# Graph network on one core: SyncE fetches one gathered column in three groups, row by row; ScalarE issues the stream loads

## The reference

```
# layer 0, transformer convolution, twice (passes c1, c2)
score = sum(q[dst] * (k[src] + e)) / 8 ; a = softmax over the edges of one dst
out   = segment_sum(a * (v[src] + e), dst) + x @ ws + bs
# layers 1 and 2, graph attention, 4 heads and 1 head (passes c3, c4, c5)
e = leaky_relu(alpha_s[src] + alpha_d[dst] (+ edge term in c3)) ; w = softmax over one dst
out = segment_sum(w * h[src], dst)
# layer 3, principal neighbourhood aggregation (pass c6)
u = h[src] + edge_attr_64 ; mean, max, min, std of u over the edges of one dst
```

## Time and profile before

| what | us |
|---|---|
| median of 3 runs | 13507.51 |
| their range | 13507.29 to 13508.39 |
| span of the profiled execution, first to last instruction | 13480.4 |
| GpSimd busy in it | 10010.5 |
| VectorE busy | 6813.4 |
| ScalarE busy | 4134.7 |

### The profile page before, as it was taken

How to read it: one execution, slowest core, us unless ns; L and a number is a source line. 1 busy time by engine, 2 the same in 40 slices (tenths; PEclk the granted TensorE clock), 3 DMA queues, 4 the chain that set the end, 5 groups by cost and what they waited for, 6 DMA issues and landing times. The chain is left out here.

```text
span 13480.4 us, 46161 instructions
## 1 busy us (share of the span) xinstructions
PE 515.1 (4%) x1768; PEld 338.5 (3%) x1768; DVE 6813.4 (51%) x10542; ACT 4134.7 (31%) x4038; POOL 10010.5 (74%) x10585
## 2 busy tenths in 40 slices
PE   3000001100000300000010000000000000000001
PEld 1000000100000200000000000000000000000000
DVE  2787776477777433333333333343333335656566
ACT  4333333233333312222212222211111113666663
POOL 7777777777777677777777777777777776777775
PEclk9999999555555655555555555555555555555555
DMA  8444443344444222222212222222222222444443
GB/s 328 128 126 119 119 119 100 95 119 119 120 120 120 57 66 63 63 61 63 60 47 59 59 58 59 59 48 57 59 59 59 58 59 82 159 159 157 159 153 121
DMA packets 919562, 1312.58 MB, mean 97 GB/s; under 512 B 600892, under 2 KB 616404, under 8 KB 906113
## 3 DMA queue, kind: packets, MB, share of 16 engines
q0 software_dynamic: 341536, 381.76, 15.7%
q10 hardware_dynamic: 85680, 537.82, 10.2%
q1 hardware_dynamic: 492209, 391.76, 10.1%
HBM read 651.09 MB, written 659.48 MB: 97 GB/s over the span
## 5 line engine op out<-in xcount | busy, mean ns | idle before, releaser
L1767 POOL DMA_INDIRECT c_y<-g_tab,srcs x4689 | 4426.0, 944 | 1429.0 <-issue 1376.9
L2200 POOL DMA_INDIRECT c_y<-h_tab,srcs x1563 | 1474.8, 944 | 510.8 <-issue 466.5
L741 POOL DMA_INDIRECT c_y<-h_tab,srcs x1563 | 1474.9, 944 | 476.3 <-issue 476.3
L1796 DVE TENSOR_TENSOR c_s<-c_y,c_ad 128x64 f32<-128x64 f32 (+1 forms) x297 | 79.1, 266 | 3450.0 <-DMA c_y<-g_tab,srcs 3448.7
L741 POOL DMA_INDIRECT first_y<-h_tab,srcs x1483 | 1399.3, 944 | 452.9 <-issue 451.7
L1879 ACT ACTIVATE c_ex<-c_de 128x64 f32<-128x64 f32 (+1 forms) x297 | 67.4, 227 | 2321.1 <-DVE c_de L1827 2320.0
L1840 DVE TENSOR_TENSOR_SCAN c_acc<-c_r,c_w_in 128x1156 f32<-128x1156 f32 (+1 forms) x297 | 753.0, 2535 | 23.2
L763 DVE TENSOR_TENSOR_SCAN c_q_all<-c_mask,c_q_in 128x408 f32<-128x408 f32 (+2 forms) x792 | 734.0, 995 | 17.8 <-issue 10.5
L806 DVE TENSOR_TENSOR_SCAN c_acc<-c_r,c_w_in 128x408 f32<-128x408 f32 (+2 forms) x792 | 731.1, 986 | 8.2
L839 ACT ACTIVATE c_q_in<-c_q_raw 128x1552 f32<-128x1552 f32 (+1 forms) x198 | 596.2, 3011 | 195.8 <-DVE c_q_in L822 195.8
L1893 ACT ACTIVATE c_row<-c_acc 128x1088 f32<-128x1088 f32 (+1 forms) x297 | 617.7, 2080 | 0.0
(11 more groups left out here) (402 smaller groups left out, 6461.6 us busy)
## 6 DMA issues: line engine op xcount, KB each, us to landing
rows_d<-c_row ACTq DMA_DIRECT2D x97, 2048.0 KB, 6.9
rows_d<-c_row ACTq DMA_DIRECT2D x291, 576.0 KB, 2.9
rows_d<-c_row ACTq DMA_DIRECT2D x194, 784.0 KB, 3.4
c_q_raw<-q_start SPq DMA_DIRECT2D x194, 776.0 KB, 4.5
q_start<-first_y SPq DMA_DIRECT2D x97, 776.0 KB, 9.0
c_y<-g_tab,srcs POOLq DMA_INDIRECT x4689, 2.5
c_y<-h_tab,srcs POOLq DMA_INDIRECT x3126, 2.5
c_ea<-in_edge_attr SPq DMA_DIRECT2D x97, 512.0 KB
```

The costliest lines, as they stand in the source:

```text
L741: nc.gpsimd.indirect_dma_start(y[:, g % NY, k, 0:D], None, h_tab, source(g, k))\
L1767: nc.gpsimd.indirect_dma_start(y[:, b, k, :], None, g_tab, source(g, k))\
L2200: nc.gpsimd.indirect_dma_start(y[:, b, k, :], None, h_tab, source(g, k))\
```

## The change

- **Fetched rows.** A new class `SyncRows`. In groups 2, 5, 8, ... 95 (slots 2 and 5 of six) the last of the 16 columns is left out of GpSimd's list; in c6 only in slot 5, so in one group of six. SyncE fetches that column with 128 DMAs, one for each row, whose byte offset in the table is in a register. It reads the offsets from a small tile `at`, 32 at a time, into registers. The tile is loaded from `places_d` in DRAM, one column ahead (in c6 after the column). VectorE waits for these rows as well (`arrived`). In c1, group 2 is still fetched by GpSimd in `begin`.
- **The table of offsets.** `begin` loads the 32 columns of `src` that are fetched this way, multiplies them by 256 and by 288 (three more VectorE steps), and stores both to `places_d`.
- **Stream loads.** All of SyncE's stream loads in the passes are issued by ScalarE, between its own steps. SyncE keeps the load of `ad_raw` at the start of c3 to c5.
- **Row buffers.** c3 to c6 use six slots where they had two, and VectorE's loop runs over six groups.

The core of the diff:

```diff
+EVERY, SYNC_K = NY // 2, GW - 1
+SYNC_SLOTS, NSYNC = [EVERY - 1, NY - 1], NGRP // EVERY
+NREG = 32
+def by_pool(g, taken):
+    return width(g) - taken.count(g % NY)
+def fill_of(slot, taken):
+    return 16 * (H2 if slot == HALVED else GW - taken.count(slot))
+    class SyncRows:
+        def load_places(self, sp, n, b):
+            sp.dma_start(self.at[b:b + 1, :], places_d[bass.ds(n * 2 + b + self.table * NSYNC, 1), :])\
+                .then_inc(self.at_loaded.h, 16)
+        def column(self, sp, n, b, used, more=True):
+            sp.wait_ge(*self.at_loaded((n + 1 if self.single else n * 2 + b + 1 - self.first) * 16))
+            if more and not self.single:
+                self.load_places(sp, n + b, 1 - b)
+            if not isinstance(n, int) or n:
+                sp.wait_ge(*used[SYNC_SLOTS[b] % 2]((n - 1) * (NY // 2) + SYNC_SLOTS[b] // 2 + 1))
+            sp.nop(nofuse=True)
+            rows = self.tab.rearrange("n f -> (n f)").bitcast(U8)
+            for lo in range(0, P, NREG):
+                _, places = nc.values_load_multi_w_load_instructions(
+                    self.at[b:b + 1, lo:lo + NREG], [mybir.EngineType.SP], min_val=0, ...)
+                for p, place in enumerate(places, lo):
+                    sp.dma_start(self.y[p:p + 1, SYNC_SLOTS[b], SYNC_K, 0:self.width].bitcast(U8),
+                                 rows[bass.ds(place, 4 * self.width)].rearrange("(a n) -> a n", a=1))\
+                        .then_inc(self.got[b].h, 16)
+            if more and self.single:
+                self.load_places(sp, n + 1, b)
+        def arrived(self, v, slot, n):
+            if slot in SYNC_SLOTS and SYNC_SLOTS.index(slot) in self.got:
+                b = SYNC_SLOTS.index(slot)
+                v.wait_ge(*self.got[b]((n + 1 - (b < self.first)) * (16 * P)))
...
 begin, SyncE
+                    sp.dma_start(src_i[:], a["src"].rearrange("(p t) -> t p", p=P)
+                                 [EVERY * GW - 1:EVERY * GW * NSYNC:EVERY * GW, :]).then_inc(src_loaded.h, 16)
...
+                sp.wait_ge(*vs.upto(len(vs)))
+                for n in range(2):
+                    sp.dma_start(places_d[n * NSYNC:(n + 1) * NSYNC, :], places[:, n, :]).then_inc(places_stored.h, 16)
+                sp.wait_ge(*places_stored(32))
 each pass, SyncE: the stream loads go
+                by_sync.all_columns(sp, weighted)
 each pass, GpSimd
-                    for k in range(width(g)):
+                    for k in range(by_pool(g, taken)):
 c3 to c6, GpSimd
-                    if g >= 2:
-                        pool.wait_ge(*weighted[b](g // 2))
+                    if g >= NY:
+                        pool.wait_ge(*weighted[g % 2]((g - NY) // 2 + 1))
 each pass, VectorE
+                    by_sync.arrived(v, slot, use)
 c1 and c2, ScalarE
+                def next_operands(n, j, w=GW):
+                    i, b = n * (NY // 2) + j // 2, j % 2
+                    act.wait_ge(*weighted[b](i))
+                    act.wait_ge(*q_turned[b](i))
+                    operands(n, j, w)
+                def group(n, j):
+                    pc = piece(n * (NY // 2) + j // 2, j % 2)
+                    turn(pc)
+                    send(piece(n * (NY // 2) + (j + 1) // 2 - 1, 1 - j % 2))
+                    next_operands(n + (j + 1) // NY, (j + 1) % NY)
+                    weights(pc)
 c3, ScalarE
+                def group(i, b, next_w=GW):
+                    weights(piece(i, b))
+                    if bd is not None:
+                        act.wait_ge(*e_scored[b](i + 1))
+                        edge_attrs(i + 1, b, next_w)
+                    send(piece(i, b))
 c6, ScalarE
+                def next_attrs(i, b, w=GW):
+                    act.wait_ge(*lifted[b](i))
+                    edge_attrs(i, b, w)
 c3 to c6
-        y = st.sb("y", [P, 2, GW, TG])
+        y = st.sb("y", [P, NY, GW, TG])
```

More of the change, by code:

```diff
@@ L187, in wide_slots, with row_slots, pass_slots @@
         return [make(f"{name}{b}", each * ((NWBLK + 1 - b) // 2)) for b in range(2)]
[L189 to L195, removed]
+    def row_slots(self, fills, taken=(), cut=0):
+        return [[self.dma(f"gathered_{slot}{part}", fill_of(slot, taken) * n - cut * part)
                  for part in range(1 + (slot == HALVED))] for slot, n in enumerate(fills)]
+    def pass_slots(self, taken, ahead=0):
+        return self.row_slots([len(range(slot, NGRP, NY)) - (slot < ahead) for slot in range(NY)], taken, CUT)
     def dma_slots(self, name, total):
@@ L360, in _ @@
                 sp.dma_start(prev_i[:], a["dst"][0:EP].rearrange("(p t) -> p t", p=P)).then_inc(dst_loaded.h, 16)
+                with nc.allow_non_contiguous_dma("one column of src in three groups"):
+                    sp.dma_start(src_i[:], a["src"].rearrange("(p t) -> t p", p=P)
+                                 [EVERY * GW - 1:EVERY * GW * NSYNC:EVERY * GW, :]).then_inc(src_loaded.h, 16)
                 sp.wait_ge(*zeroed(1))
@@ L691, in conv_edges @@
         q_loaded, e_loaded = (st.dma_slots(n, 16 * HALF) for n in ("q_loaded", "e_loaded"))
-        gathered = st.row_slots([len(range(slot, NGRP, NY)) - (slot < ahead) for slot in range(NY)], CUT)
+        taken = SYNC_SLOTS
+        gathered, by_sync = st.pass_slots(taken, ahead), SyncRows(st, y, h_tab, D, 0, ahead // EVERY)
         q_turned, weighted, row_ready = (st.piece_slots(n) for n in ("q_turned", "weighted", "row_ready"))
@@ L770, in step @@
                     for part in halves(gathered[slot], pc):
-                        v.wait_ge(*part((use + (slot >= ahead)) * ((8 if slot == HALVED else 16) * GW) - missing(pc)))
+                        v.wait_ge(*part((use + (slot >= ahead)) * fill_of(slot, taken) - missing(pc)))
+                    by_sync.arrived(v, slot, use)
                     v.wait_ge(*e_loaded[pc.slot](pc.load * 16 + 16))
@@ L874, in _ @@
                 weights(piece(0, 0))
[L875 to L884, removed]
+                for j in range(1, NY):
+                    group(0, j)
+                with act.Fori(1, NGRP // NY) as n:
+                    for j in range(NY):
+                        group(n, j)
                 for before, pc in zip([piece(HALF - 2, 1)] + LASTS, LASTS):
@@ L1728, in gat_edges @@
             eadded = st.sem("eadded", NPIECE)
-        gathered = st.gather_halves(f"gathered_{'first' if tag in ('c1', 'c2', 'c3') else 'later'}_", 8 * GW * HALF)
+        taken = SYNC_SLOTS
+        gathered, by_sync = st.pass_slots(taken), SyncRows(st, y, g_tab, TG, 1)
         weighted, row_ready, den_in = (st.piece_slots(n) for n in ("weighted", "row_ready", "den_in"))
@@ L1793, in step @@
                     w_heads = w_cur.rearrange("p (h j) t -> p h j t", h=H)
-                    for part in halves(gathered[pc.slot], pc):
-                        v.wait_ge(*part(pc.load * (8 * GW) + 8 * GW - missing(pc)))
+                    for part in halves(gathered[slot], pc):
+                        v.wait_ge(*part((use + 1) * fill_of(slot, taken) - missing(pc)))
+                    by_sync.arrived(v, slot, use)
                     v.tensor_tensor(s0[:, :, 0:w], ys[:, :, D:D + H].rearrange("p t h -> p h t"), ad[:, :, cols],
@@ L2166, in pna_edges @@
         e_loaded = st.dma_slots("e_loaded", 16 * HALF)
-        gathered = st.gather_halves(f"gathered_{'first' if tag in ('c1', 'c2', 'c3') else 'later'}_", 8 * GW * HALF)
+        taken = SYNC_SLOTS[1:]
+        gathered, by_sync = st.pass_slots(taken), SyncRows(st, y, h_tab, D, 0, single=True)
         row_stored = st.store_slots("row_stored")
```

162 lines of the change are left out of this document (85 added, 77 removed).

## The result

The changed kernel takes 13300.6 us (median of 4 runs, 13275.6 to 13302.8); the kernel before, beside it on the same chip, 13507.4 (4 runs, 13504.6 to 13508.4). The ratio is 0.9843, with a 95% interval of 0.9829 to 0.9857. The medians differ by 206.8 us, the profiled spans (13480.4 and 13273.9) by 206.5; 214.5 had been forecast, and 13293 as the time. The time of a run lies 1.7 us above its own span (13275.6 and 13273.9), so of the 27.1 us between the span and the median before, some 25 are the difference between one execution and another; here too the profiled execution is the fastest, 25 us under the median.

The account below looks back on a forecast made before the run. GpSimd's gathers, 1.2485 us a column, were taken to bound the kernel. 218.5 us saved less 4 us of setup gave 214.5, so 13266 us against the profiled span, 13293 with 27.1 us added for the median; range 13280 to 13880.

Parts of the forecast that it names:

- S: SyncE's time for one fetched column: 52.5 + 4 + 0.7 = 57.2 us, bounds 41.5 and 75.0.
- The gain: GpSimd's list in c1 to c6: 175 columns fewer at 1.2485 us, 218.5 us saved.
- Setup: Setup stage: SyncE's 4096-word load of one src column in three groups adds 4 us, bounds 0 and 15.
- A row: One-row DMA on SyncE: 0.34 + 0.06 + 0.01 = 0.41 us, bounds 0.32 and 0.52; 128 rows 52.5 us.
- rival D: Both register instructions per row make SyncE the bound in five passes: 1590 us more, 14883 us; chance 0.20 with milder forms.
- Register loads: SyncE reading 128 places into registers, four times 32: 4 us a column, between 0.1 and 7.7.
- The limit: c1 to c5: GpSimd needs 58.7 us for 47 columns; a fetch within that costs nothing.
- under its wait for GpSimd: VectorE's one more wait, in a third of its steps, was to lie under its existing wait for GpSimd.
- The other sign: Sign of being right: SyncE's idle time ended by VectorE's weighted in each column.
- Rival C: c1 and c2: ScalarE's loads hold SyncE three times 3.4 us a column, adding 542 us, 13835 us; chance 0.12.
- The bound from above: c6: SyncE has 117 us for a fetched column, so S does not matter even at 75 us.
- The price of a miss: c1 to c5: each us of S above 58.7 costs 159 us.

Follow-up runs that it names:

- the one with exchanged pieces: Changed kernel with c1/c2 edge features in 128 pieces (not 2048) to a spare tile, c6's store in 4096 pieces (not 128): 13275.6 us, one run.

## Why the prediction was right

The mechanism was the one forecast: GpSimd's pace sets the passes, 175 columns less at 1.2485 us, and the fetch lies beside. The time was met to 0.06%, the gain to 4% (206.8 us of 214.5). Two terms of S were not, their errors had opposite signs, and S left out two more. The lower bound of S was also added up wrongly: 41.0 + 0.1 + 0.7 is 41.8, not 41.5; nothing rests on it.

**The gain.** 218.5 us were forecast off GpSimd's list, 214 measured between the first and the last gather. Of that, 2.3 us came back behind the last gather of c1 and 3.9 behind that of c6 (a wait of 25.7 us where it was 21.8), where the last group waits for VectorE and its store. Setup cost 1.2 us (c1's first gather starts at 391.8 instead of 390.6), not the 4 that I took; its bounds of 0 and 15 hold it. 214 - 6.2 - 1.2 = 206.6; measured 206.5. So what was left out are the ends of the passes, 6.2 us, which no row of before had suggested; they are as long without any fetch, so they aren't SyncE's doing. With all columns back on GpSimd the wait of c1 is 19.8 us and that of c6 21.1, so the one comes with the moved loads or buffers and the other with GpSimd's shorter list.

**A row.** 0.317 us was measured, outside my bounds of 0.32 to 0.52 and well below the 0.41 taken. I had the MOVE right (one, no FUSED_REGOPS, so rival D's premise is refuted), but took 0.34 us as the issue from loads of 2 KB. The one-row load with its 0.28 us was the nearest row of all and pointed lower; the real figure is 0.225. 128 rows are 40.6 us, not 52.5.

**Register loads.** Four of 2.12 us are 8.5 us, above my upper bound of 7.7. The bound assumed one MOVE for a value, 0.06 us, and forgot that the load can have a part beside it that doesn't depend on the number. The Trainium skill ("DMA: Bandwidth & Descriptors", "Latency and other measured facts") gives a floor of about 600 ns. The trace doesn't contradict a floor (the shortest load took 0.97 us, for 16 values), but as a price it is far off: four floors are 2.4 us, less than a third of what was measured; the price follows the number of values in the two sizes tried.

**What S left out.** Once in two columns the loop goes back to its start and 2.4 us pass without an instruction (in the timeline above, 3054.39 to 3057.22 between a fetch and the next load, against 0.3 us inside the body); in c1 it is 3.7 to 5.2 us. And 3.7 to 4.5 us a column in c1 and c2 go to row issues that take 1 us instead of 0.225 while ScalarE's DMAs move. So S came out as 40.6 + 8.5 + 4 + 1.2, and some 3 us of loads and waits, 57.6 in c1 and 57.2 in c2, in place of 57.2. The sum was right by luck: the rows were 12 us too dear, and 4.5 us of register loads, the branch and the slow issues that I had left out made up for them.

**The limit.** 58.7 us was right for c2 to c5, where c2 has 1.5 us of margin and c3 to c5 some 5: a period there is 56.5 us, of which 2.9 are waits (276.5 us over 96 columns), so SyncE's own work is 53.6. In c1 it was wrong: there it is 57.5, since five groups lie ready, and the change has nothing to spare. A forecast that had counted this would have given c1 a chance of its own to lose. The forecast's "under its wait for GpSimd" failed there: VectorE waits for SyncE's rows in 27 columns of 31. That it costs nothing measurable is shown by the kernel without fetches and by the one with exchanged pieces. The other sign, that idle time of SyncE ends by `weighted` in each column, came in 57 columns of 96 in c3 to c5, in all but one of c6, and in 3 of 63 in c1 and c2.

**Rival C.** The hold-up does reach from ScalarE's queue to SyncE's. The Trainium skill ("DMA: Bandwidth & Descriptors", "Queues, rings and completion order") has it that the two engines have no descriptor generator of their own, and the trace agrees in the sign. What failed in C is the size: not 3.4 us for each load of 2048 pieces, but some 1.4 us a group with all of ScalarE's DMAs counted, because SyncE isn't stopped, it goes on at about 1 us a row. The other way nothing is seen. ScalarE's own issue of that load takes 1.084 us, where SyncE's took 0.38 us, but it takes 1.075 us too in the kernel in which SyncE issues no row, so SyncE's rows aren't the cause, and what is stays open:
```profile
L900 ACTq DMA_DIRECT2D c_y<-in_edge_attr x98: 457/1075/1120, 2488.0 to 4388.9; - x98
```
I had read the earlier trace rows as weak evidence against a hold behind the 2 MB store: a single issue, with none behind it. In the changed kernel, where rows follow each other, the issues behind the same store are slow for 6.4 us, and 3.4 of them are lost.

**The bound from above.** In c6 the forecast said that S doesn't matter even at 75 us, and the measured 63.4 us in a period of 118 agrees (the 117 us of the forecast should have been 95 x 1.2485 = 118.6). Tried at three groups it did matter, which shows why a column in six was the right share there.

**The price of a miss.** 159 us for each us of S stands: 9.1 us more of register loads (9.3 in the periods of c1 and c2, 10.2 in c3 to c5), less a margin of some 1 us in c1, 1.5 in c2 and 5 in c3 to c5, gave 974 us, which is 6.1 x 159, and in c6 3.7 us above the limit are 118 us over 32 columns; less the 20 us of GpSimd's 16 columns 98 were due, and 79 showed.

## What to carry to other kernels

Work taken off the engine that sets the pace is worth its full price only as long as the engine that gets it has less to do per period than the first one; so reckon that period part by part for every stage, with the work that each stage finds ready, since a share that fits one stage (one column in three) is a loss in another (c6) and on the edge in a third (c1). Look at the releasers of the receiving engine's waits, not at its busy share: 10.9 us of waiting over two passes says that the margin is used up, and so do 27 waits of VectorE for SyncE's rows in c1. And an estimate that comes out right on the sum may do so from errors that cancel, so compare the terms too before the next column is moved.

## What the runs showed of the hardware that I had not expected

- A one-row DMA whose address is in a register is issued in 0.225 us on SyncE and 0.235 on ScalarE; with its MOVE a row goes out every 0.317 us, for 256 B as for 288.
- A register load takes 2.12 us for 32 values and 1.23 for 16 on SyncE; on ScalarE 3.13 for 32 in the middle of its compute (at least 2.15). Unused ones don't reach the trace at all.
- Behind a store of 2 MB on ScalarE, SyncE's issues are slow for 6.4 us and a register load takes 4.98 us; with the same bytes in 4096 pieces it takes 7.40 us, and a fetch in c6 69.9 us instead of 63.4.
- One DMA of 4096 single words in the setup stage held SyncE's next issue 12.65 us; the forecast's guess was 8:
```profile
L436 SPq DMA_DIRECT2D q_start<-first_y x98: 332/332/12652, 11.6 to 248.1; - x98
```
- Behind the backward branch of a loop whose body holds 256 row DMAs SyncE stands idle for 2.4 us (2.37 to 2.79 in c3 to c5, 3.7 to 5.2 in c1); in the short loop of the setup stage for 0.12. In c6, with 128 row DMAs, it is 0.23 us. It isn't the body's length alone: with loads of 16 places c6 has the same loop in two kernels, and there it is 0.20 us in the one and 3.0 in the other.
